# A selective-scan layer on one core: unit 0's products from tokens put at the end of TensorE's set-up, unit 0's first steps in another order, and the loads of the set-up's end spread out

## What is computed

```python
ada = silu(c) @ Wada.T + bada;  shift, scale, gate = split(ada, 3)
x_ssm = ln(x, g1, b1) * (1 + scale) + shift;  skip = x_ssm
x_ssm = ln(x_ssm, g2, b2)
mz = x_ssm @ Wz.T + bz;  act_mx = silu(x_ssm @ Wx.T + bx)
z1 = ssm(mz @ Wc1.T + bc1, ...)                 # forward
z2 = flip(ssm(flip(mz @ Wc2.T + bc2), ...))     # backward
out = (act_mx * z1 + act_mx * z2) @ Wf.T + bf + skip
return x + gate * out

# ssm(u): dlt, Bm, Cm = split(u @ Wdbc.T);  delta = softplus(dlt @ Wdt.T + bdt)
#   h[t] = exp(delta*A) * h[t-1] + delta * Bm * u;  y = sum_n(h * Cm) + u * Dp
```

## Time and profile before

| | us |
|---|---|
| median of 3 runs | 3278.92 |
| lowest and highest | 3277.81, 3281.28 |
| profiled execution | 3282.95 |
| its span | 3281.1 |
| end of the set-up, first scan | 230.43, 251.66 |

### The profile page before, as it was taken

How to read it: one execution, slowest core, us unless ns; L and a number is a source line. 1 busy time by engine, 2 the same in 40 slices (tenths; PEclk the granted TensorE clock), 3 DMA queues, 4 the chain that set the end, 5 groups by cost and what they waited for, 6 DMA issues and landing times.

```text
span 3281.1 us, 54891 instructions
## 1 busy us (share of the span) xinstructions
PE 2988.6 (91%) x19924; PEld 2373.0 (72%) x19924; DVE 3014.0 (92%) x2006; ACT 2679.4 (82%) x5153; POOL 2900.1 (88%) x1280
## 2 busy tenths in 40 slices
PE   8978999899998999899999999899999999899999
PEld 5756666667767666678877766678778666677789
DVE  2739999999999999999999999999999999999994
ACT  1448999988888999987788999987877999988772
POOL 0428999999999999999999999999998999999993
PEclk9989999999999999999999999999999999999999
DMA  5765334644475333645575434645566333645463
GB/s 223 248 230 187 130 119 135 225 160 156 167 250 198 132 130 127 224 151 157 162 246 186 135 118 137 222 140 165 167 217 209 122 131 130 228 137 165 155 199 111
DMA packets 207053, 560.40 MB, mean 171 GB/s; under 512 B 20200, under 2 KB 66472, under 8 KB 202560
## 3 DMA queue, kind: packets, MB, share of 16 engines
q1 hardware_dynamic: 203424, 538.01, 48.9%
q10 hardware_dynamic: 2208, 10.49, 0.9%
q0 software_dynamic: 1152, 8.39, 0.6%
HBM read 476.19 MB, written 80.63 MB: 170 GB/s over the span
## 4 chain that ended last, share of the span: by engine, by line
PE 50%; ACT 20%; DVE 12%; issue 10%; DVEq 0%; ACTq 0%
PE y L880 14%; PE slot L891 10%; PE mb L851 9%; ACT abuf L1129 8%; PE mb L964 6%; DVE hbuf L1322 6%; ACT slot L1191 3%; DVE hbuf L1331 3%; PE mb L861 3%; PE slot L903 3%; DVE slot L1322 3%; ACT dec L1191 2%; ACT soft L1085 2%; PE mb L922 1%; PE mb L957 1%
## 5 line engine op out<-in xcount | busy, mean ns | idle before, releaser
L1235 POOL TENSOR_TENSOR hbuf<-hbuf,cres 128x1024 f32<-128x1024 f32 x704 | 1664.6, 2378 | 143.4 <-DVE hbuf L1322 143.4
L1230 POOL TENSOR_TENSOR bst<-bst,du 128x1024 f32<-128x1024 f32 x512 | 1221.0, 2385 | 46.3 <-DVE du L1266 46.3
L1322 DVE TENSOR_TENSOR_SCAN hbuf<-dec,slot 128x1024 f32<-128x1024 f32 x512 | 1164.9, 2275 | 39.0 <-PE slot L903 27.1
L880 PE MATMUL y<-ident,hbuf 128*128 128x128 f32 x8192 | 1016.1, 273 | 0.0
L880 PEld LDWEIGHTS y<-ident,hbuf 128*128 128x128 f32 x8192 | 924.5, 141 | 104.5 <-issue 104.0
L1129 ACT ACTIVATE abuf<-dut,bt 128x128 f32<-128x128 f32 x3072 | 964.5, 387 | 0.0
L1322 DVE TENSOR_TENSOR_SCAN slot<-slot,bst 128x1024 f32<-128x1024 f32 x320 | 728.3, 2276 | 23.0 <-ACT slot L1191 22.1
L1191 ACT ACTIVATE slot<-delta,par 128x1024 f32<-128x1024 f32 x512 | 568.2, 1110 | 198.1 <-DVE hbuf L1331 185.1
L1191 ACT ACTIVATE dec<-delta,par 128x1024 f32<-128x1024 f32 x512 | 584.1, 1141 | 115.5 <-DVE hbuf L1322 114.9
L891 PE MATMUL slot<-ident,abuf 128*128 128x128 f32 x3072 | 408.4, 276 | 170.4 <-ACT abuf L1129 161.0
L891 PEld LDWEIGHTS slot<-ident,abuf 128*128 128x128 f32 x3072 | 339.0, 141 | 302.8 <-ACT abuf L1129 243.9
(11 more groups left out here) (156 smaller groups left out, 2363.2 us busy)
## 6 DMA issues: line engine op xcount, KB each, us to landing
bst<-bc_s SPq DMA_DIRECT2D x512, 512.0 KB, 4.0
cres<-bc_s SPq DMA_DIRECT2D x128, 512.0 KB, 6.8
wzs<-wz_s SPq DMA_DIRECT2D x64, 256.0 KB, 4.1
yf_s<-yrd SPq DMA_DIRECT2D x32, 512.0 KB, 5.3
ybuf<-yf_s SPq DMA_DIRECT2D x32, 512.0 KB, 4.9
yg_s<-ybuf SPq DMA_DIRECT2D x31, 512.0 KB, 4.4
si_s<-silu SPq DMA_DIRECT2D x28, 512.0 KB, 6.1
silu<-si_s SPq DMA_DIRECT2D x28, 512.0 KB, 5.4
```

What stands on the lines that cost most here:

```text
L880: last = nc.tensor.matmul(y[:, j * P:(j + 1) * P], hbuf[:, q % HR, j * P:(j + 1) * P], ident[:], start=False, stop=(q % N == N - 1), is_tr ...
L1230: nc.gpsimd.tensor_tensor(bst[:, i % BR, :], bst[:, i % BR, :], du[:, k % 2, :], ALU.mult).then_inc(pool_b, 1)
L1235: nc.gpsimd.tensor_tensor(hbuf[:, q % HR, :], hbuf[:, q % HR, :], cres[:, q % N, :], ALU.mult).then_inc(pool_prod, 1)
L1322: nc.vector.tensor_tensor_scan(h[:, ::step], decays[:, ::step], inflows[:, ::step], 0.0, ALU.mult, ALU.add).then_inc(scanned, 1)
```

## The change

Four things. TensorE's products for unit 0 (delta, the transposes of B, z) are its last work of the set-up, in a function `first_unit`; for that the PSUM tensors are made once for both blocks, and the set-up's eight banks are halves of them. ScalarE loads no table at the scan block's start. In unit 0, ud comes before the diagonals, VectorE and not ScalarE copies dut, and the second set of diagonals is written behind the second decay. In SyncE's queue tokens are stored one fold later, the tokens for unit 0 are loaded in folds 11 and 12, dl in 13, the four bst one by one from fold 14 on, and wproj is stored in halves.

```diff
-        ps = [ctx.enter_context(nc.psum_tensor(f"ps{i}", [P, TC], fp32)) for i in range(8)]
+        ps = [t[name][:, half * TC:(half + 1) * TC] for name, half in (
+            ("y", 0), ("slot1", 0), ("slot1", 1), ("slot0", 0), ("y", 1), ("mb", 0), ("slot0", 1), ("mb", 1))]
...
-                if f - 1 in TURN_AT:
-                    store_tokens(TURN_AT.index(f - 1))
+                if f - 2 in TURN_AT:
+                    store_tokens(TURN_AT.index(f - 2))
...
+                if f in (FP + 2, FP + 3):
+                    load_first_tokens(f - FP - 2)
                 if f == FP + 4:
-                    load_first_products()
-                    for h in range(2):
-                        sp.wait_ge(xnt_first[h], 16 * DT)
-                        sp.dma_start(xn0[:, h], scratch["xn"][h]).then_inc(xn_in[h], 16)
+                    load_first_delta()
+                if f >= FP + 5:
+                    load_first_b(f - FP - 5)
+            store_tokens(NC - 2)
             store_folded(NF - 3)
             store_tokens(NC - 1)
+            for i in range(NF - FP - 5, BR):
+                load_first_b(i)
+            sp.wait_ge(proj_ready[0], 2)
+            sp.dma_start(scratch["wproj"][:, 0:DT * RD], ...)
...
+            def first_unit():
+                pe.wait_ge(wdt_in[0], 16)
+                pe.wait_ge(dl_in, 48)
+                pe.wait_ge(dbo_ready, 2)
+                pe.wait_ge(xnt_ready, DT * NC)
+                for h in range(2):
+                    nc.tensor.matmul(t["mb"][:, h * TC:(h + 1) * TC], wdt[:, 0, :], dl[:, h * TC:(h + 1) * TC],
+                                     start=True, stop=True).then_inc(t["dps_mm"], 1)
+                pe.wait_ge(wcz_ready, 2 * NF)
+                pe.wait_ge(bcz_ready, NF)
+                for j in range(ET):
+                    last = nc.tensor.matmul(t["slot1"][:, j * N:(j + 1) * N], dl[R:R + N, j * P:(j + 1) * P],
+                                            ident[R:R + N, R:R + N], start=True, stop=True, is_transpose=True)
+                last.then_inc(t["bt_mm"], 1)
+                pe.wait_ge(wz0_in, 16)
+                for h in range(2):
+                    pe.wait_ge(xn_in[h], 16)
+                    for i in range(DT):
+                        last = nc.tensor.matmul(t["y"][:, h * TC:(h + 1) * TC], wz0[:, i * P:(i + 1) * P], xn0[:, h, i, :],
+                                                start=(i == 0), stop=(i == DT - 1))
+                    last.then_inc(t["z_mm"], 1)
...
-            pe.wait_ge(ones_ready, 1)
-            delta_product(0)
-            turn_b(0)
-            for h in range(2):
-                z_part(0, h, range(DT))
...
-            nc.scalar.preload_act_table_set("natural_log_exp_and_others")
...
             softplus_end(0)
+            for h in range(2):
+                skip_half(0, h)
             copy_bt(0)
             make_diagonal(0, 0)
-            for h in range(2):
-                skip_half(0, h)
-            for h in range(2):
-                copy_dut(0, h)
-            make_diagonal(0, 1)
...
-                    if c == 1 and k > 0 and k % ET == 0:
+                    if c == 1 and k % ET == 0:
                         make_diagonal(k // ET, 1)
...
+            for h in range(2):
+                dve.wait_ge(dut_mm, h + 1)
+                nc.vector.tensor_copy(dut[:, half(h)], mb[h]).then_inc(dut_ready, 1)
```

More of the change, by code:

```diff
@@ L154, in load_first_products, with load_first_tokens, load_first_b @@
                 sp.dma_start(dl[R:R + N, :], scratch["bc"][0, 0, 0:N, :]).then_inc(dl_in, 16)
-                for i in range(BR):
-                    sp.dma_start(bst[:, i, :], scratch["bc"][0, 0, POOLED[i], :].partition_broadcast(P)).then_inc(b_in[i], 16)
+            def load_first_tokens(h):
+                sp.wait_ge(xnt_first[h], 16 * DT)
+                sp.dma_start(xn0[:, h], scratch["xn"][h]).then_inc(xn_in[h], 16)
+            def load_first_b(i):
+                sp.dma_start(bst[:, i, :], scratch["bc"][0, 0, POOLED[i], :].partition_broadcast(P)).then_inc(b_in[i], 16)
             for f in range(NF):
@@ L177, in _ @@
                     load_first_units()
+                if f in (FP + 2, FP + 3):
+                    load_first_tokens(f - FP - 2)
                 if f == FP + 4:
-                    load_first_products()
-                    for h in range(2):
-                        sp.wait_ge(xnt_first[h], 16 * DT)
-                        sp.dma_start(xn0[:, h], scratch["xn"][h]).then_inc(xn_in[h], 16)
+                    load_first_delta()
+                if f >= FP + 5:
+                    load_first_b(f - FP - 5)
+            store_tokens(NC - 2)
             store_folded(NF - 3)
             store_tokens(NC - 1)
+            for i in range(NF - FP - 5, BR):
+                load_first_b(i)
+            sp.wait_ge(proj_ready[0], 2)
+            sp.dma_start(scratch["wproj"][:, 0:DT * RD], wproj[:, 0].rearrange("p k r -> p (k r)")).then_inc(wproj_out, 16)
             for g in range(NF - 2, NF):
@@ L187, in _ @@
             sp.wait_ge(proj_ready[1], 2)
-            sp.wait_ge(proj_ready[0], 2)
-            sp.dma_start(scratch["wproj"], wproj[:].rearrange("p a k r -> p (a k r)")).then_inc(wproj_out, 16)
+            sp.dma_start(scratch["wproj"][:, DT * RD:2 * DT * RD], wproj[:, 1].rearrange("p k r -> p (k r)")).then_inc(wproj_out, 16)
             sp.dma_start(scratch["dbias"], dbias[:]).then_inc(wproj_out, 16)
@@ L469, in _ @@
                     project(c)
+            first_unit()
 KINDS = "EVAVEVAPAVAPAPAV"
@@ L532, in ssm_kernel @@
         gate = t["gate_sb"]
-        y = ctx.enter_context(nc.psum_tensor("y", [P, S], fp32))
-        slot = [ctx.enter_context(nc.psum_tensor(f"slot{i}", [P, S], fp32)) for i in range(2)]
-        mbw = ctx.enter_context(nc.psum_tensor("mb", [P, S], fp32))
+        y, mbw = t["y"], t["mb"]
+        slot = [t["slot0"], t["slot1"]]
         mb = [mbw[:, 0:TC], mbw[:, TC:S]]
@@ L545, in ssm_kernel @@
         y_out, yg_out, out_out, si_out = (sem(n) for n in ("y_out", "yg_out", "out_out", "si_out"))
[L546 to L549, removed]
+        dps_mm, z_mm, bt_mm = (t[n] for n in ("dps_mm", "z_mm", "bt_mm"))
+        turned, dut_mm, scaled, bt_ready, dut_ready = (sem(n) for n in (
+            "turned", "dut_mm", "scaled", "bt_ready", "dut_ready"))
+        mx_mm, ytr_mm, ud_mm, summed, proj_mm = (sem(n) for n in (
+            "mx_mm", "ytr_mm", "ud_mm", "summed", "proj_mm"))
         soft_step, soft_ready, ud_ready, decay_ready, y_read, sig_step, sig_ready = (sem(n) for n in (
@@ L1369, in build @@
             t[name] = ctx.enter_context(nc.sbuf_tensor(name, shape, fp32))
-        for name in ("dl_in", "ones_ready", "wzs_in"):
+        for name in ("y", "slot0", "slot1", "mb"):
+            t[name] = ctx.enter_context(nc.psum_tensor(name, [P, S], fp32))
+        for name in ("dl_in", "ones_ready", "wzs_in", "dps_mm", "z_mm", "bt_mm"):
             t[name] = ctx.enter_context(nc.semaphore(name))
```

4 lines of the change are left out of this document (2 added, 2 removed).

## The result

The changed kernel takes 3264.7 us (3260.72 to 3267.34), beside it the kernel before 3281.28 (3277.81 to 3281.92): a ratio of 0.9951, interval 0.9938 to 0.9964, so faster by 12 to 20 us. The sign was right and most of the mechanism was there. Read in the profile at the fourth scan, 18.7 us were gained of the 28.8: TensorE's folds end 8.0 us later than forecast, the end of SyncE's queue costs 1.1 more and the first steps 0.9 more. Of the rest of the gap to 3250, 2.4 us lie in the starting point: the kernel before took 3281.28 beside the changed one, and the forecast set out from 3278.92.

The account below looks back on a forecast made before the run. VectorE was taken to bound the 64 units, so only time before the fourth scan counted: 17.5 us from an earlier seam plus 11.3 from the first steps, 28.8, took 3278.92 to 3250 us, range 3245 to 3264.

Parts of the forecast that it names:

- The loop passes everything on: 64-unit loop: runs at VectorE's pace, about 47 us a unit, so an earlier start moves everything behind it equally.
- Part 1, first half: Set-up, SyncE's queue: wct waits of 1.2 and 4.37 go, with 3.1 of slow clock: 8.7 us gained.
- Part 1, second half: Set-up, wct 12 and 13: the other two waits and slow stretches nearly go, 1.5 us remaining.
- The upper end on record: Set-up, wct 12 and 13: the most that remaining waits and a slow stretch were to cost, 7 us.
- The rule that spoke against part 1: Set-up DMA: engines go round-robin between queue rows, so other queues stretch SyncE's; wct waits cost 7 us instead of 1.5.
- Part 2, the products: End of set-up, TensorE: unit 0's products take 9.1 us at the high clock, hidden behind SyncE's tail by 1.8.
- Part 2, the tail: End of set-up, SyncE: old chain 20 us earlier plus 2.5 for two bst loads; the seam moves by 17.5.
- Part 3: First steps of unit 0: fourth scan 18.9 us behind the seam instead of 30.2, 11.3 gained.
- The table load: ScalarE, start of scan block: covered before, it would stand uncovered in the new order; its row is 1.28 us.
- A: Rival, set-up: waits for wct change place, losing up to 7 us or all 13 of the rest; 3256 to 3262, chance 0.24.
- B: Rival, middle of set-up: all four wct waits stay, total gain 8.8 us, 3270; chance 0.06.
- D: Rival, loop: another phase adds a wait of about 0.6 us per unit, 38 us more, 3288; chance 0.02.

Follow-up runs that it names:

- e3: The changed kernel with unit 0's two token loads moved behind the requests for wct 14 and 15: 3252.24 us, ratio 0.9914.
- e4: The changed kernel with the stores of token chunks 3 and 4 moved from folds 12 and 13 to behind the requests for wct 14 and 15: 3257.18 us, ratio 0.9928.
- e10: The changed kernel with GpSimd's 1.05 MB store of xsk chunk 5 moved from between the requests for wct 12 and 13 to the end: 3263.12 us, one execution.
- e5: e3 with all four loads of bst in folds 14 and 15, none between the last token store and dbias: 3250.3 us, ratio 0.9913.
- e8: e3 with ScalarE's table load put back at the start of the scan block: 3257.99 us, one execution.
- e2: The changed kernel with the old SyncE queue, keeping the products in the set-up and the new first steps: 3272.87 us, ratio 0.9979.
- e9: e5 with four extra products of 512 columns on TensorE behind the seam: 3252.1 us, ratio 0.9912.
- e11: The changed kernel with the stores of token chunk 3 one fold later, behind the request for wct 13: 3259.09 us, one execution.

## Why the prediction was wrong, step by step

- **The loop passes everything on.** Right, as far as the traces can tell: from the fourth scan to the end it is 3016.9 to 3022.4 us in all thirteen, in no order with the change.
- **Part 1, first half, 8.7 us.** Right: the fold that ended (L401, L412) at 164.86 ends at 156.15, 8.71 earlier, and the waits of 1.2 and 4.37 are gone.
- **Part 1, second half: the step that failed.** "I take 1.5 for all, since most landings have slack." It is 9.5, since the whole gain was 12.1 of 21.6: waits of 2.33 and 3.37 (5.7), and nearly all of the rest in the slow folds behind both (3.4 against e3). The upper end on record, 7, was also too low, and so was the wait at wct 12, 0 to 1.5. What was wrong in it is the picture of the queue. I charged wct 13 with the 4.5 MB from the first token load to it, at 421 GB/s, 10.6 us, and with up to 5 us for other queues: landed by 168 at the latest. It landed at 173.5. From the load's issue at 150.58 to there it is 22.9 us, with the window

```profile
150.60:173.50 22.90, 17.24 (x93) 15.00 (x91) 16.75 (x34) 7.76 (x15) 14.23 (x13) 0.92 1.01 358
```

so some 8.2 MB passed, at 358 GB/s: the rate was a little lower, the bytes were nearly double. The megabytes of the other queues were in the upper end; the token stores issued behind wct 13 were nowhere in the sum. And I let SyncE issue wct 13 when the fold allowed it: the token stores held it for 5.2 us and the folded weight's for 3.2, and wct 13 went out at 160.9 instead of 155.8 as in e4. e3 shows that with the loads out of these folds the sum as written down comes true, 3252 against 3250. That it is so close is in part luck: e3's folds end 1.5 us earlier than forecast and its tail is 1.25 longer.
- **The rule that spoke against part 1.** The row-by-row sharing between queues (the Trainium skill, DMA: Bandwidth & Descriptors, "Queues, rings and completion order") was taken as a reason for the upper end. The end was nearer the truth, but e10 gives the store on the other queue only 0.8 to 1.4 of 5.7 us. The same section says that completion isn't in the order of issue. The trace agrees: the first token store was issued at 151.58, behind wct 12, and landed after 7.5 us, at 159.1, ahead of wct 12 at 160.0. I didn't draw it into the sum.
- **Part 2, the products.** 9.1 forecast, 9.6 measured, at clock 1.00; hidden behind SyncE's tail by 3 us.
- **Part 2, the tail.** Mis-sized by 1.1: from the last token store to the seam it was 11.8, forecast 14.3 (2.5 more), measured 15.4 (3.6 more). Two loads of 0.52 MB cost more than their bytes at 421 GB/s; without them (e5) dbias lands 4.2 earlier. That SyncE's tail would set the seam, and that these loads stretch it, was right (e5).
- **Part 3.** Right in size: 11.3 forecast, 10.4 measured. The low clock came as forecast (3.79 for the diagonal products), the second set of diagonals is hidden (the fourth scan is 7.85 behind the first, forecast 7.9). The 1 us missing is ahead of the first scan. Both turns of du together took 2.0 where one was put at 1.0 at most, and VectorE's copies came 0.9 apart, so the second copy ends 8.1 behind the seam and not 7.5; from there to the scan it is 3.9 and not 3.5.
- **The table load.** That it would have stood bare in the new order, at its row's 1.28, was right (e8).
- **The rivals.** A was the right one, with 0.24: the waits for wct change place. With the measured folds alone it would be at 3258, inside its 3256 to 3262; above that lie the longer tail (1.1), the first steps (0.9) and the kernel before's 2.4. B's premise, that all four waits stay, is e2's by construction, and there TensorE's end is at 230.4 as B had it (230.6); its seam at 232.4 by the longer tail was not met by any run. D: no sign of another phase in the loop.

The lowest ratios of all runs are e9's, e5's and e3's, 0.9912, 0.9913 and 0.9914, which the times can't tell apart; e5 has the earliest seam.

## What to carry to other kernels

When transfers are spread over a queue that also carries what an engine waits for, count per stretch all that is issued close to the awaited request, ahead of it and behind it, and let the issuing engine be held up too: a rate from the busiest window and the bytes ahead gave 1.5 us where 9.5 came. Price a wait with what it does to the clock behind it, too: with 5.7 us of waits and a low clock behind them the folds ended 4.0 us later than with 5.1 us behind which the clock stayed up. Spreading a heap helps only if its pieces land in stretches with room; here folds 14 and 15 had it (e3, e4), folds 12 and 13 had not. Work moved in front of a seam is free up to the moment at which the last store lands, so that moment has to be costed with the same change in it.

## What had not been expected of the hardware

- A request's landing can depend on what the same engine issues behind it: wct with the same ahead of it landed after 9.0 us without, 13.1 us with eight stores of 0.26 MB behind it; another after 6.4 and 8.9. These are single traces, and up to 1.4 us of such a difference can be there without the stores. Without a token load ahead, four stores behind left it at 4.8 and 5.5.
- Issuing stretches with load: four stores took 2.29 us of SyncE with an empty queue, up to 9.54 in a loaded one (DMA share 1.02 from 161.7 to 171.2 us).
- Waits of 1.25, 1.52 and 2.36 us in e11 were followed by a clock of 1.00, those of 2.33 and 3.37 in the changed kernel by 0.55 and 0.52.
- A table load of the set that is already there cost 1.28 us and nothing more.
